# Attention with exponential features: the output bias of the first row tile is added behind, not ahead of, the last feed-forward tile's factors

## The reference, cut to what matters

```python
# x: (8, 2048, 512); 16 heads of 32; omega: (32, 128)
qkv = x @ Wqkv + bqkv
q, k, v = heads(qkv)
phi = lambda t: exp(t @ omega - 0.5 * sum(t * t))      # 128 features a head
kv, k_sum = phi(k)^T @ v, sum_n phi(k)
attn = (phi(q) @ kv) / (phi(q) @ k_sum + 1e-6)
x = layernorm(x + attn @ Wout + bout)                  # bout: the output bias
y = x @ weight^T + pooled(x) @ disha                   # pooled: 8 blocks of 64 summed
x = layernorm(x + y)
```

## Time and profile before

| what | value |
|---|---|
| median of three runs | 2395.49 us |
| profiled execution | 2395.51 us |
| its span, first to last instruction | 2393.7 us |
| granted TensorE clock, mean | 0.998 |
| PE / DVE / ACT / POOL busy | 98% / 82% / 53% / 12% |
| share of the chain that ended last | PE 87%, DVE 7%, issue 3%, ACT 2% |
| bias additions (L976) | 128, 1325 ns each in the mean |
| pow of the factors (L987) | 128, 549 ns each |

### The profile page before, as it was taken

The page is one execution under the profiler, slowest core; times in us unless marked ns, Lnnn a source line. Parts: engine busy times, 40 slices in busy tenths (PEclk is TensorE's granted clock), DMA queues, the critical chain, the costliest instruction groups (busy, mean ns, idle before and its releaser), DMA issues.

```text
span 2393.7 us, 55214 instructions
## 1 busy us (share of the span) xinstructions
PE 2343.8 (98%) x21224; PEld 1325.2 (55%) x21224; DVE 1956.4 (82%) x3751; ACT 1268.2 (53%) x2281; POOL 286.7 (12%) x390
## 2 busy tenths in 40 slices
PE   8999999999999999999999999999999999999997
PEld 4545555555555555555555555555555555555554
DVE  6778887888888888887888878888778888788776
ACT  4555555555555555555555555555555555555443
POOL 0001111011111011111011110111110111100221
PEclk9999999999999999999999999999999999999999
DMA  6322332323323323323323233233233232232231
GB/s 209 90 74 71 108 80 82 94 82 94 101 71 99 94 68 108 87 76 96 89 85 104 73 92 95 76 100 98 66 106 90 72 108 76 86 77 59 73 102 50
DMA packets 160277, 213.11 MB, mean 89 GB/s; under 512 B 19376, under 2 KB 119824, under 8 KB 156048
## 3 DMA queue, kind: packets, MB, share of 16 engines
q1 hardware_dynamic: 159440, 208.53, 31.3%
q10 hardware_dynamic: 576, 1.05, 0.1%
HBM read 73.19 MB, written 33.55 MB: 45 GB/s over the span
## 4 chain that ended last, share of the span: by engine, by line
PE 87%; DVE 7%; issue 3%; ACT 2%; SPq 0%; DMA 0%; DVEq 0%; POOL 0%; POOLq 0%; ACTq 0%
PE bank_y L459 24%; PE bank_a L459 24%; PE bank_x L459 12%; PE bank_kf L524 4%; PE bank_qf L578 4%; PE kv_ps L550 3%; PE bank_nm L609 3%; PE bank_x L626 3%; PE bank_nm L626 1%; DVE q_feat_lo L843 1%; PE bank_nm L614 1%; PE kv_ps L556 1%; PE bank_x L486 1%; PE bank_a L486 1%; PE kv_ps L459 1%
## 5 line engine op out<-in xcount | busy, mean ns | idle before, releaser
L706 ACT ACTIVATE q_feat<-bank_qf 128x512 f32<-128x512 f32 x512 | 305.8, 597 | 183.9 <-PE bank_qf L578 183.7
L836 DVE TENSOR_TENSOR k_feat_lo<-k_feat 128x512 bf16<-128x512 f32 x512 | 367.2, 722 | 43.3 <-ACT k_feat L696 43.3
L696 ACT ACTIVATE k_feat<-bank_kf 128x512 f32<-128x512 f32 x512 | 306.0, 598 | 169.7 <-PE bank_kf L524 137.5
L843 DVE TENSOR_TENSOR q_feat_lo<-q_feat 128x1024 bf16<-128x1024 f32 x256 | 313.3, 1224 | 12.3 <-ACT q_feat L706 10.7
L987 POOL TENSOR_TENSOR rstd<-mean_var,minus_half 128x1 f32<-128x1 f32 x128 | 70.3, 549 | 1648.1 <-DVE mean_var L919 1648.1
L976 POOL TENSOR_TENSOR rows<-rows,bias_out 128x512 f32<-128x512 f32 x128 | 168.2, 1325 | 442.1 <-DMA rows<-x 440.2
L524 PE MATMUL bank_kf<-omega_s,stack_k 98*128 98x128 f16 x1920 | 185.8, 219 | 3.1 <-ACT k_feat L696 2.7
L550 PE MATMUL kv_ps<-v_both,k_feat 128*128 128x65 f16 (+1 forms) x2048 | 181.3, 190 | 5.9 <-DVE k_feat_lo L836 5.3
L578 PE MATMUL bank_qf<-stack_q,omega_s 98*128 98x256 f16 x960 | 183.7, 272 | 1.2 <-ACT q_feat L706 1.2
L556 PE MATMUL kv_ps<-v_both,k_feat_lo 128*128 128x33 f16 x2048 | 182.6, 179 | 0.0
L524 PEld LDWEIGHTS bank_kf<-omega_s,stack_k 98*128 98x128 f16 x1920 | 136.1, 97 | 77.6 <-issue 23.5
(11 more groups left out here) (206 smaller groups left out, 5147.7 us busy)
## 6 DMA issues: line engine op xcount, KB each, us to landing
rows<-x SPq DMA_DIRECT2D x128, 256.0 KB, 2.9
out<-rows SPq DMA_DIRECT2D x128, 256.0 KB, 2.1
xt_f<-xt SPq DMA_DIRECT2D x31, 1024.0 KB, 5.0
stack_k<-t_hi_k SPq DMA_DIRECT2D x240, 128.0 KB, 2.4
stack_q<-t_hi_q SPq DMA_DIRECT2D x240, 128.0 KB, 2.4
stack_k<-t_lo_k SPq DMA_DIRECT2D x120, 128.0 KB, 2.4
stack_q<-t_lo_q SPq DMA_DIRECT2D x120, 128.0 KB, 2.4
stack_q<-t_hi_k SPq DMA_DIRECT2D x16, 128.0 KB, 2.5
```

Of the source, the lines that this page charges most:

```text
L696: nc.scalar.activation(k_feat[:, i % 2, :], bank_kf[:, :], ACT.Exp, scale=1.0 / WS).then_inc(S["k_exp"], 1)
L706: nc.scalar.activation(q_feat[:, 2 * pair:2 * pair + 2, :], bank_qf[:, :].rearrange("p (e n) -> p e n", e=2), ACT.Exp, scale=1.0 / WS).the ...
L836: v.tensor_tensor(k_feat_lo[:, u, :], k_feat[:, u, :], k_feat_hi[:, u, :], ALU.subtract).then_inc(S["kfl"], 1)
L843: v.tensor_tensor(q_feat_lo[:, at, :], q_feat[:, at, :], q_feat_hi[:, at, :], ALU.subtract).then_inc(S["qfl"], 2)
```

## The change

```diff
@@ -976,7 +976,7 @@
                 nc.gpsimd.tensor_tensor(rows[:, t, :], rows[:, t, :], bias_out[:, :],
                                         ALU.add).then_inc(S["xb_done"], 1)
 
-            BIAS_BEHIND = (("NM", 0), ("NM", 2), ("QF", 12), ("NM", 4))
+            BIAS_BEHIND = (("NM", 2), ("NM", 3), ("QF", 12), ("NM", 4))
 
             def step(b, c, kind, i, what):
                 kA, j = 4 * b + c, 4 * b - 4 + c
```

## The result

The changed kernel takes 2406.53 us, the kernel before 2397.68 us (medians of 20 runs each): 8.9 us apart. The ratio by all runs is 1.0033, 95% interval 1.0027 to 1.0040, so about 0.33% slower. That is less than the 0.5% named in the prediction, but clear of noise with this many runs, and above the range of 2393.0 to 2405.3.

A forecast was written before the change was run, and what follows sets the result against it. TensorE was taken to bound the kernel. To the profiled 2395.51 us came -2.0 (freed place at KFIN), +3.9 (five lost turns) and +0.6 (two odd pairs), +2.5 in sum: forecast 2398.0, range 2393.0 to 2405.3.

The forecast's parts named there:

- the beginning of the prediction: TensorE makes up 87% of the chain; POOL idles at least 3.50 us before FF3's factors, so tile 0 never holds them.
- (a): Tile 0's addition moves behind the factors, still 4.9 us ahead of its first reader, r1 (L906): cost 0.
- (c): Behind the factors, tile 1's addition follows tile 0's and holds attn (L891): DVE 0.8 us later, bounds 0 and 1.23.
- the rival in which it loses it: At NM2, den (L884) loses its turn to tile 1's addition, DVE 1.23 us late: +9.3 us, 2404.8; chance 0.13.
- (d): At KF2's k_feat_lo (L836), DVE's 0.8 us delay is swallowed in 17 slots; five of eight others lose their turn.
- (e): At NM4 on PE, a lost turn costs 1.23 less 0.45 us slack, 0.78 us, five times: 3.9 us.
- (b): Ahead of the factors, the freed place ends holds on L867 and L869 in two KFIN slots: gain 2.0 us.
- The third rival: Loads of tiles 2 and 3 land 0.8 us later along with DVE, nothing is swallowed: +14 us, 2409.5; chance 0.05.
- The five lost turns: Five slots where k_feat_lo (L836) comes too late to run between tiles 2 and 3's additions: 3.9 us together.

The follow-up runs named there:

- e5: Kernel before plus a VectorE memset of about 0.8 us behind NM2's attn in the steady slots; 2410.38 us, ratio 1.0047 to before.
- e1: Changed kernel, but tile 1's addition waits for NM2's attn in the steady slots; 2393.76 us, ratio 0.9978 to before.
- e8: Changed kernel, but tile 3's addition waits for KF2's k_feat_lo in the steady slots; 2400.69 us, ratio 1.0012 to before.
- e2: Kernel before with the additions of tiles 2 and 3 cut to one column of 512; 2387.49 us, ratio 0.9947 to before.
- e3: Changed kernel with the additions of tiles 2 and 3 cut to one column of 512; 2393.30 us, ratio 0.9974 to before.
- e9: Changed kernel, steady slots' additions of tiles 0 to 3 waiting for KF0's k_feat_lo, QF9's q_feat_lo, KF2's k_feat_lo, QF13's q_feat_lo; 2382.82 us, ratio 0.9931.

## Why the prediction was wrong

*What bounds, and the queue (the beginning of the prediction, parts (a) and (c)).* Right. The factors were never held by tile 0: POOL's idle time ahead of FF3's pow is 8.36 us now in the slot shown. attn is held by about 0.8 us in each of the 27 slots, as read from the one row of four additions that bore on it. den does not lose its turn; the rival in which it loses it, which was the strict reading of the rule in the Trainium skill, "SBUF — State Buffer", "Who interferes with whom", did not happen. Its time of 2404.8 us came close to the measured one, but by a way that was not taken: den takes 0.49 us in the row above, where it would have needed 1.7.

*The two halves of the change, set apart.* Four kernels make a square: tile 0's addition in its old or its new place, DVE in time or 0.7 to 0.8 us late behind NM2. Medians in us:

| | DVE in time | DVE late |
|---|---|---|
| tile 0 in front | before, 2397.68 | e5, 2410.38 |
| tile 0 behind the factors | e1, 2393.76 | changed, 2406.53 |

The lateness costs about 13 us in either row, the new place gives about 4 us in either column. The prediction had 4.5 (3.9 and 0.6) for the first and 2.0 for the second. So what was mis-sized above all is the lateness, by parts (d) and (e) below. By the slots of the profiled executions the lateness costs 13.3 and 10.1 us, and the place gives 2.5 and 5.7.

*Part (b), the free place in front.* The mechanism was right and the term too small, by the medians. I counted the two slots with a visible hold on KFIN, 2.0 us. Between e5 and the changed kernel, which have the same A, A + B differs by 5.7 us, 5.2 of it in the six slots that lead to KFIN (446.5 against 441.3 us). Between before and e1 these six slots differ by 1.7 us: in the kernel before only two additions met KFIN, and in e5 five did.

*Part (d), "the delay is swallowed".* This is the step that failed. I held the pair's start and end fixed and moved only k_feat_lo. But holding works both ways: q_feat_lo reads two tensors from SBUF too, and 0.8 us later it covers the pair's start. The trace of before had it: in the 17 slots q_feat_lo ended only 0.1 to 0.5 us ahead of the pair (0.18 in the slot shown above), a distance that I had not looked at. So the pair ends when q_feat_lo lets it, not when the loads land, and 0.45 of the 0.79 us gets through in the slot shown above (10.74 against 10.29), 0.34 us in the mean of the 17. The third rival, that the pair moves with DVE, had the right effect and the wrong cause; I excluded it by looking at the loads alone. e8 shows it from the other side: with k_feat_lo let through ahead of tile 3, 5.8 of the 12.8 us come back although attn is still held.

*Part (e), the price of lateness.* 0.45 us were taken off as slack at NM4. e2 and e3 show none: in all ten kernels a plain slot is longer by what the last q_feat_lo is later, from +19.36 and 72.22 us (e9) over +19.71 and 72.58 (e3) to +20.10 and 72.96 (changed). In the mean of the plain slots, q_feat_lo came 0.35 us later and the slot became 0.34 us longer. The gate at NM4 has slack up to +19.83; the gates behind it have none from +19.4 on. The five lost turns, which made up most of my sum, are not most of what was measured: 22 of the 26 slots grew. Nor was one lost as described, since no second pair of the changed kernel starts between +7.7 and +8.5. But in three of the five slots (those of 988.43, 1279.76 and 1643.63 us) the pair comes at +7.52 to +7.58 now, k_feat_lo ends at +10.74 or +10.75 instead of +9.51 to +9.75, and the slot is 0.73 to 0.94 us longer, 2.4 us together. My price of 0.78 us came close to that by luck. It took DVE to be 1.23 us later at the last q_feat_lo, but the rows shown with the prediction already had less: from the end of that k_feat_lo to the end of q_feat_lo DVE needs 9.40 us in the slot of 1134.10 and 9.78 us in that of 403.80. So DVE does have about 0.4 us of idle time on the way, where (c) says that it has none, and the slack that I took off at NM4 is not there.

*The sum again, by A and B.* A grew by 6.9 us, where parts (d) and (e) had 4.5. B grew by 0.7, where part (b) had it shrink by 2.0: the gain at KFIN, 0.6 and 1.0 us in the two slots counted, is there, but the gates behind NM4 took more. Together 7.6 us in the slots, against a measured difference of the medians of 8.9 (6.5 to 9.6 by the interval); the remainder is within the spread of single executions, whose starts alone differ by 2.5 us.

*Not settled.* Why the second pair starts anywhere from +7.2 to +9.9, with the loads issued in the same order each time, was not tried. Nor was what makes the lower clock appear early in some executions.

## What to carry to other kernels

Where two engines hold each other up, the holder can be held as well: a delay of one moves the other's end too. So list which instructions of both can be held before calling a delay absorbed. Before counting a wait's slack as free, look at what the late engine makes next: slack at the first gate is worth nothing where the next gate has none. A small addition on GpSimd is not free by being off the chain; its place relative to VectorE's two-input instructions was worth 24 us here, from the changed kernel to e9, with all the same work.

## What the runs showed of the hardware

A GpSimd addition of 128x512 float32 and VectorE's instructions with two SBUF inputs held each other up, in both directions, until the one that came first was done: attn took 1.21 instead of 0.42 us, k_feat_lo 1.74 instead of 0.68 us, and the addition, when VectorE came first, 1.67 us in e8 and 1.59 us in e1 instead of 1.27. A VectorE instruction that waited behind one of two adjacent additions went in between them: den ended 0.03 us behind tile 0's addition in all 27 slots of the changed kernel and did not wait for tile 1's, and in the kernel before k_feat_lo split the second pair, which then took 2.95 instead of 2.50 us. VectorE's instructions with one input from PSUM ran beside additions at their usual times (L906 0.68 us, 59 times in e9), and so did its statistics of rows (L788, 0.69 us) and the reciprocal of 128x8 (L887, 0.20 us).
